# Two fp4 feed-forwards: VectorE's chains of x and of h woven into one another, x one turn ahead

## The chip, the cores and the metric

One core of one Trainium2 chip runs the whole program. The time is device microseconds of one execution. Of the kernel before there are three runs: 4086.76, 4089.36 and 4089.8 us, median 4089.36. Everything computes in fp32, except where the reference rounds to fp4.

## The reference

The program is a chain of eight sublayers on a residual stream of 8 sequences x 256 tokens x 128 channels, each with a layer norm in front. Two of the eight, the sixth and the last, are the same fp4 feed-forward with the same weights:

```python
def fp4_quant_dequant(x):                       # blocks of 16 along the last dim
    scale = max(max(abs(xb)) / 6.0, 1e-12)
    xn = xb / scale
    idx = searchsorted(_MID, abs(xn))            # 7 midpoints of the grid 0 .5 1 1.5 2 3 4 6
    return _GRID[idx] * sign(xn) * scale

gate = fp4_linear(x, w_gate)    # 128 -> 352, both operands rounded by blocks of 16
up   = fp4_linear(x, w_up)      # 128 -> 352
out  = fp4_linear(silu(gate) * up, w_down)       # 352 -> 128
```

Here x is the normed stream; out is added to the stream. The six other sublayers are not touched by the change.

## The kernel before, in words

The stream lies in SBUF for the whole program, channels on the 128 partitions (net.xT), its normed form likewise (net.zT). `fp4_ffn` goes over the 8 sequences ("images") one after the other, 256 tokens each, in a pipeline of stages that is written out by hand: each engine has one instruction list, in the order in which `iteration(n, stages)` appends it, and every engine waits for the others, and for its own earlier results, by semaphores. An engine's list is strictly in order.

The work of one image:

1. **x comes in** (TensorE, L2246): two transposes of net.zT bring tokens to the partitions, into x_in, one half of the bank p_x.
2. **The x chain** (VectorE, `round_x`): eight instructions, each of which waits for the one in front: maximum of each block (L2345), scale (L2348), reciprocal (L2350), the factor against ties (L2352), the quotients into SBUF (L2354, tile x_a) and once more in place in PSUM (L2356), their exponents (L2358), and from those the magic number (L2360) that rounds when it is added and subtracted.
3. **Rounding x** (GpSimd): moved = a + magic (L2130), q = moved - magic (L2132), xq = q x scale (L2137).
4. **x back** (TensorE, L2252): two transposes into x_back, the other half of p_x; ScalarE copies them to xqT (L2300).
5. **Up** (TensorE, L2260): four matmuls of 352 columns, two into the banks p_gate and two into p_up. ScalarE takes SiLU of the gate (L2305).
6. **The h chain** (VectorE): the product h = SiLU(gate) x up of 704 columns (L2366), block maximum (L2368), scale, reciprocal and tie factor of 44 columns (L2379 to L2383), quotients (L2385, tile h_a), exponents (L2387), magic number (L2389); each waits for the one in front. GpSimd makes h_moved and h_q (L2130 and L2132 again); VectorE scales back into hq (L2373, `scale_back`).
7. **Down** (TensorE): six transposes of hq into p_h and p_last (L2270), copied by ScalarE (L2310, L2311), then a matmul that adds the residual (L2275) and three of the weights (L2277) into the other half of p_last; ScalarE copies the sum to net.xT (L2315, `add`).

In turn n VectorE does: x chain of image n, product and maximum of n-1, scale-back of n-2, the rest of the h chain of n-1. GpSimd: x of n, then h of n-1. TensorE: x back of n, x in of n+1, transposes of h of n-2, up of n, down of n-2. ScalarE: `add` of n-3, copy of x of n, copies of h of n-2, SiLU of n. x in of n+1 waits for ScalarE's copy of x_back (both lie in p_x). The transposes of h wait for the `add` of the image before (both lie in p_last). A single scale tile per chain makes the next scale wait for the scale-back of the image before.

In front of the first call the weights are rounded and transposed; both calls begin with a layer norm. What follows the calls (the next norm, the store) needs the last image.

Of the kernel before, what the change touches and what calls it, by code (L numbers as in the profile page):

```python
# [20 lines left out]
ACT = mybir.ActivationFunctionType  # L21
ALU = mybir.AluOpType
# [2172 lines left out]
def fp4_ffn(net, tag):  # L2195
# [12 lines left out]
    with Mem(nc, tag) as m:  # L2208
# [6 lines left out]
        x_ = {n: m.sb(f"x_{n}", [P, w]) for n, w in (("scale", NX), ("inv", NX), ("a", L), ("magic", L), ("moved", L), ("q", L))}  # L2215
        h_ = {n: m.sb(f"h_{n}", [P, w]) for n, w in (("a", H2), ("expo", H2), ("magic", H2), ("moved", H2), ("q", H2))}
        p_x = m.ps("p_x", [P, BANK])
# [5 lines left out]
        x_in, x_back, h_last, p_out = p_x[:, 0:L], p_x[:, L:2 * L], p_last[:, 0:L], p_last[:, L:2 * L]  # L2223
# [3 lines left out]
        h_am, h_inv0, h_inv, h_scale = (own(L + 2 * NX + i * NHB, NHB) for i in range(4))  # L2227
# [6 lines left out]
        def pipeline(iteration):  # L2234

            for n in range(B + 3):
                iteration(n, tuple(stage for stage in (1, 2, 3, 4) if 0 <= n - stage + 1 < B))

        @block.tensor
        def _(pe):  # L2240
            def turn_in(n):
                if n >= B:
                    return
                need(pe, s["xqT_ready"], n)
                for t in range(2):
                    ins = nc.tensor.transpose(x_in[:, t * P:(t + 1) * P], net.zT[:, n, t * P:(t + 1) * P], net.ident[:, :])  # L2246
                ins.then_inc(s["z_turned"], 1)

            def turn_back(n):
                pe.wait_ge(sx["out"], n + 1)  # L2250
                for t in range(2):
                    ins = nc.tensor.transpose(x_back[:, t * P:(t + 1) * P], xq[:, t * P:(t + 1) * P], net.ident[:, :])  # L2252
                ins.then_inc(s["xq_turned"], 1)
# [26 lines left out]
            def iteration(n, stages):  # L2280
                if 1 in stages:
                    turn_back(n)
                    turn_in(n + 1)
                if 3 in stages:
                    turn_h(n - 2)
                if 1 in stages:
                    up(n)
                if 3 in stages:
                    down(n - 2)

            turn_in(0)
            pipeline(iteration)
# [3 lines left out]
        def _(act):  # L2296
            def copy_x(n):
                act.wait_ge(s["xq_turned"], n + 1)
                need(act, s["up_ready"], 2 * (n - 1))
                nc.scalar.activation(xqT[:, n % 2, :], x_back, ACT.Copy).then_inc(s["xqT_ready"], 1)  # L2300
# [16 lines left out]
            def iteration(n, stages):  # L2317
                if 4 in stages:
                    add(n - 3)
                if 1 in stages:  # L2320
                    copy_x(n)
                if 3 in stages:
                    copy_h(n - 2)
                if 1 in stages:
                    silu(n)

            pipeline(iteration)

        @block.gpsimd
        def _(pool):  # L2330
            def iteration(n, stages):
                if 1 in stages:
                    fp4_round(pool, nc.gpsimd, x_, sx, n + 1)
                    fp4_times_scale(pool, nc.gpsimd, x_, sx, n + 1, xq[:, :])
                if 2 in stages:
                    fp4_round(pool, nc.gpsimd, h_, sh, n)

            pipeline(iteration)

        @block.vector  # L2340
        def _(dve):
            def round_x(n):
                done = n + 1
                dve.wait_ge(s["z_turned"], done)
                nc.vector.tensor_reduce(x_am, in_blocks(x_in), AX.X, ALU.max, apply_absolute_value=True).then_inc(sx["am"], 1)  # L2345
                need(dve, sx["out"], n)
                dve.wait_ge(sx["am"], done)
                nc.vector.tensor_scalar(x_["scale"][:, :], x_am, 1.0 / 6.0, 1e-12, ALU.mult, ALU.max).then_inc(sx["scale"], 1)  # L2348
                dve.wait_ge(sx["scale"], done)
                nc.vector.reciprocal(x_inv0, x_["scale"][:, :]).then_inc(sx["inv0"], 1)  # L2350
                dve.wait_ge(sx["inv0"], done)
                nc.vector.tensor_scalar(x_["inv"][:, :], x_inv0, TIES_DOWN, None, ALU.mult).then_inc(sx["inv"], 1)  # L2352
                dve.wait_ge(sx["inv"], done)
                nc.vector.tensor_tensor(in_blocks(x_["a"][:, :]), in_blocks(x_in), per_block(x_["inv"][:, :]), ALU.mult).then_inc(sx["a"], 1)  # L2354
                dve.wait_ge(sx["a"], done)
                nc.vector.tensor_tensor(in_blocks(x_in), in_blocks(x_in), per_block(x_["inv"][:, :]), ALU.mult).then_inc(sx["turned_a"], 1)  # L2356
                dve.wait_ge(sx["turned_a"], done)
                nc.vector.tensor_scalar(x_expo.bitcast(U32), x_in.bitcast(U32), EXPONENT, None, ALU.bitwise_and).then_inc(sx["expo"], 1)  # L2358
                dve.wait_ge(sx["expo"], done)
                nc.vector.tensor_scalar(x_["magic"][:, :], x_expo, 1.0, MAGIC, ALU.max, ALU.mult).then_inc(sx["magic"], 1)  # L2360

            def multiply(p):
                done = p + 1
                dve.wait_ge(s["gated"], done)
                dve.wait_ge(s["up_ready"], 2 * done)
                nc.vector.tensor_tensor(h[:, :].rearrange("p (t f) -> p t f", t=2), gate[:, :, :], p_up[:, :, 0:DF], ALU.mult).then_inc(s["h_ready"], 1)  # L2366
                dve.wait_ge(s["h_ready"], done)
                nc.vector.tensor_reduce(h_am, in_blocks(h[:, :]), AX.X, ALU.max, apply_absolute_value=True).then_inc(sh["am"], 1)  # L2368

            def scale_back(r):  # L2370
                need(dve, s["h_turned"], r)
                dve.wait_ge(sh["q"], r + 1)
                nc.vector.tensor_tensor(in_blocks(hq[:, :]), in_blocks(h_["q"][:, :]), per_block(h_scale), ALU.mult).then_inc(sh["out"], 1)  # L2373

            def scale_h(p):
                done = p + 1
                need(dve, sh["out"], p)
                dve.wait_ge(sh["am"], done)
                nc.vector.tensor_scalar(h_scale, h_am, 1.0 / 6.0, 1e-12, ALU.mult, ALU.max).then_inc(sh["scale"], 1)  # L2379
                dve.wait_ge(sh["scale"], done)  # L2380
                nc.vector.reciprocal(h_inv0, h_scale).then_inc(sh["inv0"], 1)
# [238 lines left out]
```

## Time and profile before

| | |
|---|---|
| median of three runs | 4089.36 us |
| the profiled execution's own time | 4093.68 us |
| its span, in which the rows below count | 4091.9 us |
| busy: TensorE, VectorE, ScalarE, GpSimd | 3767.2, 3550.8, 3327.1, 3075.6 us |
| granted TensorE clock, mean | 0.965 of full |
| first fp4 call, first transpose to last residual copy | 3838.55 to 3927.51 us |
| second fp4 call, to its last residual copy | 3995.00 to 4084.27 us |

A row of the timeline has its start on the span's clock, its duration, the engine (PE is TensorE, DVE VectorE, ACT ScalarE, POOL GpSimd), the line of the kernel, the operation, the tile written and the tiles read, and shapes as partitions x columns. Tile names are cut: fp_p_own is the bank p_own, which holds the small tiles of both chains. In square brackets stands how long the engine had been idle and what released it. Merged rows give a count (x4) and the time from the first start to the last end.

### The profile page before, as it was taken

What the parts mean: (1) busy time and instruction counts of PE and PEld (TensorE: products, weight loads), DVE (VectorE), ACT (ScalarE), POOL (GpSimd) and SP (SyncE); (2) the same over time, 40 slices, a digit from 0 to 9 for tenths busy, and PEclk for the clock granted to TensorE, in tenths of its full rate; (3) what the DMA queues carried; (4) which work ended last, traced back from release to release, by engine and by line L of the source; (5) the groups of instructions that cost most, each with busy time, mean ns of one, the idle gap of its engine ahead of it and who ended that gap; (6) DMA issues with size and microseconds to landing.
All of it is one profiled execution on the core that took longest, in us unless ns stands there. A gap on an engine that the chain in (4) does not pass through costs nothing. (4 is left out here: it accounts for less than half of the span.)

```text
span 4091.9 us, 139809 instructions
## 1 busy us (share of the span) xinstructions
PE 3767.2 (92%) x51875; PEld 2247.0 (55%) x51875; DVE 3550.8 (87%) x11427; ACT 3327.1 (81%) x10473; POOL 3075.6 (75%) x4007
## 2 busy tenths in 40 slices
PE   6888889999999999999867999999999999996676
PEld 2333346666666666666553666666666666663464
DVE  7999989999999999999487999999999999975646
ACT  6888689999999999999515999999999999993122
POOL 3999788888888888888396888888888888762314
PEclk8999999999999999999898999999999999997887
DMA  1000111111112111111002111111111111110000
GB/s 30 1 1 1 48 25 34 44 34 39 44 28 54 31 36 49 26 36 34 12 1 64 26 36 46 29 50 35 31 48 35 44 31 39 31 26 3 6 3 11
DMA packets 78603, 122.65 MB, mean 30 GB/s; under 512 B 26024, under 2 KB 47204, under 8 KB 77924
## 3 DMA queue, kind: packets, MB, share of 16 engines
q1 hardware_dynamic: 77924, 113.71, 10.7%
q8 instruction: 413, 6.77, 0.7%
q14 instruction: 266, 2.18, 0.2%
HBM read 35.56 MB, written 1.05 MB: 9 GB/s over the span
## 5 line engine op out<-in xcount | busy, mean ns | idle before, releaser
L1131 POOL TENSOR_TENSOR local_qk<-local_qk,local_rb 128x512 f32<-128x512 f32 x768 | 973.2, 1278 | 88.5 <-DVE local_rb L1541 88.5
L1427 ACT ACTIVATE local_pr<-local_tb,local_nmax 128x96 f32<-128x96 f32 x3072 | 1010.5, 379 | 24.6 <-DVE local_nmax L1560 14.1
L1237 PE MATMUL local_pj<-local_wqkv,local_xs 128*64 128x512 f32 x3072 | 814.1, 609 | 21.5 <-DVE local_rb L1541 8.3
L1164 POOL TENSOR_TENSOR local_pr<-local_pr,local_rsum 128x384 f32<-128x384 f32 x768 | 623.0, 828 | 274.4 <-DVE local_rsum L1567 274.4
L1560 DVE CUSTOM_DVE_ANT_0 local_tb<-local_tb,local_mask,local_rinv 128x96 f32<-128x96 f32 x3072 | 772.6, 319 | 14.5 <-PE local_tb L1262 14.0
L1427 ACT ACTIVATION_READ_ACCUMULATOR local_pr<-local_tb,local_nmax 128x1 f32 x3072 | 753.1, 245 | 0.0
L1538 DVE TENSOR_TENSOR local_qk<-local_pj,local_rope 128x512 f32<-128x512 f32 x768 | 517.4, 674 | 113.7 <-ACT local_sq L1410 108.5
L1548 DVE TENSOR_REDUCE local_ss<-local_sq 128x8 f32<-128x512 f32 x768 | 521.8, 680 | 32.0 <-ACT local_sq L1410 32.0
L1410 ACT ACTIVATE local_sq<-local_pj 128x512 f32<-128x512 f32 x768 | 491.6, 640 | 55.6 <-PE local_pj L1237 55.3
L1541 DVE TENSOR_TENSOR local_rb<-local_pj,local_rope 128x512 f32<-128x512 f32 x768 | 523.0, 681 | 3.4 <-POOL local_qk L1131 3.4
L1286 PEld LDWEIGHTS local_ob<-local_prT,local_v 128*64 128x64 f32 x12288 | 413.9, 138 | 137.8 <-issue 55.4
L1435 ACT ACTIVATE local_prT<-local_tb 128x512 f32<-128x512 f32 x768 | 457.2, 639 | 5.7 <-PE local_tb L1273 5.7
L1560 DVE DVE_READ_ACCUMULATOR2_ANT local_nmax<- 128x1 f32 x3072 | 433.1, 141 | 0.0
L1286 PE MATMUL local_ob<-local_prT,local_v 128*64 128x64 f32 x12288 | 428.2, 223 | 3.4 <-DVE local_oT L1577 1.8
L1248 PE MATMUL local_pj<-local_wqkv,local_xs 128*64 128x512 f32 x1536 | 410.5, 613 | 4.4 <-DVE local_rb L1541 4.2
L1137 POOL TENSOR_TENSOR local_qk<-local_qk,local_rinv 128x512 f32<-128x512 f32 x384 | 400.5, 1044 | 0.0
L1262 PEld LDWEIGHTS local_tb<-local_kT,local_qT 64*64 64x64 f32 x12288 | 271.5, 133 | 202.9 <-ACT local_pr L1427 78.4
L783 POOL TENSOR_TENSOR mamba_scan_drive<-mamba_u,mamba_scan_b_all 128x512 f32<-128x512 f32 x256 | 319.8, 1271 | 52.3 <-ACT mamba_scan_b_all L753 48.7
L1311 PE MATMUL local_fb<-local_oT,local_wo 128*64 128x256 f32 x3072 | 348.0, 379 | 0.0
L1262 PE MATMUL local_tb<-local_kT,local_qT 64*64 64x96 f32 x12288 | 329.2, 250 | 3.3 <-ACT local_pr L1427 1.8
L1301 PEld LDWEIGHTS local_tb<-net_ident,local_qk 64*128 64x128 f32 x6144 | 231.5, 139 | 183.1 <-issue 82.3
L1350 PE MATMUL local_fb<-local_xn,local_w 128*64 128x256 f32 x2304 | 308.5, 389 | 10.3 <-DVE local_g L1601 5.7
(461 smaller groups left out, 7252.6 us busy)
## 6 DMA issues: line engine op xcount, KB each, us to landing
local_v<-local_v SPq DMA_DIRECT2D x288, 256.0 KB, 3.8
local_wqkv<-L_ffn_Wqkv_dram SPq DMA_DIRECT2D x72, 256.0 KB, 2.8
local_wo<-L_ffn_Wo_dram SPq DMA_DIRECT2D x12, 512.0 KB, 4.0
local_w<-L_ffn_W_dram SPq DMA_DIRECT2D x12, 341.0 KB, 2.9
mamba_parts<-mamba_in_low SPq DMA_DIRECT2D x24, 64.0 KB, 2.0
local_w<-L_ffn_W_dram SPq DMA_DIRECT2D x12, 128.0 KB
y_dram<-store_xtok SPq DMA_DIRECT2D x4, 256.0 KB, 2.8
local_oT<-rope_dram SPq DMA_DIRECT2D x2, 256.0 KB, 2.8
```

The costliest lines, as they stand in the source:

```text
L1131: nc.gpsimd.tensor_tensor(qk[:, u, :], qk[:, u, :], rb[:, u % 2, :], ALU.add).then_inc(s["summed"], 1)
L1164: nc.gpsimd.tensor_tensor(at, at, view(rsum[:, k // 2, k % 2, 0:1], [[1, 4], [0, KW]]), ALU.mult).then_inc(s["weighted"], 1)
L1237: ins = nc.tensor.matmul(bank[own, :], xs[:, par, u // 4 * P + own.start:u // 4 * P + own.stop], wqkv[:, dep % 2, u % 4 * BANK:(u % 4 + 1) ...
L1262: ins = nc.tensor.matmul(sc[h][low * QB:(low + 1) * QB, i * KW:(i + 1) * KW], qT[own, par, p, q:q + QB], kT[own, par, p, q:q + KW], start= ...
L1286: ins = nc.tensor.matmul(ob[h * DH:(h + 1) * DH, i * P + low * QB:i * P + (low + 1) * QB], v[:, par, V_BLOCK[2 * t + low], 2 * (4 * half + ...
L1410: nc.scalar.activation(sq[:, u % 2, :], projection_bank("rotated", u)[:, :], ACT.Square).then_inc(s["squared"], 1)
L1427: ins = nc.scalar.activation(pr[:, (NU * c + k) % PR_RING, i, WIN:WIN + KW], scores[:, i * KW:(i + 1) * KW], ACT.Exp, scale=-1.0, bias=nma ...
L1435: nc.scalar.activation(prT[:, kk % PT_RING, low, :], pair_of_banks("probs", kk)[low][:, :], ACT.Copy).then_inc(s["probs_copied"], 1)
L1538: nc.vector.tensor_tensor(heads8(qk[:, u, :]), heads8(bank[:, :]), cosines, ALU.mult)
L1541: nc.vector.tensor_tensor(rb[:, u % 2, :].rearrange("p (h a c) -> p h a c", a=2, c=DH // 2), swapped, sines, ALU.mult).then_inc(s["rotated ...
L1548: nc.vector.tensor_reduce(ss[:, par, 8 * u:8 * u + 8], heads8(sq[:, u % 2, :]), AX.X, ALU.add).then_inc(s["summed_sq"], 1)
L1560: ins = nc.vector.tensor_tensor_reduce(at, at, mask[:, k // 4, :], rinv[:, par, head:head + 1], 3.0e38, ALU.add, ALU.min, nmax[:, k, i:i + 1])
```

## The change

- **VectorE**: each step becomes a function of its own. Step by step an instruction of the h chain of image n-1 is followed by one of the x chain of image n+1; the scale-back of n-2 ends the turn. The x chain of image 0 runs alone ahead of the loop. Each step still waits for its own chain's previous step by the same semaphores; new waits guard the tiles that are reused: h quotients wait until h_moved of the image before has been made (`sh["moved"]`), h_magic until its q has (`sh["q"]`), likewise in the x chain.
- **GpSimd**: in turn n x of image n, then h of image n-2. h of an image waits for the scale-back of the one before; xq for the transposes back of the one before.
- **TensorE**: in turn n x in of n+1, transposes of h of n-3, x back of n, up of n, down of n-3. x in waits for the exponents of the image before in place of ScalarE's copy; x back waits for SiLU of the image before.
- **ScalarE**: copies of h of n-3, copy of x of n, SiLU of n, `add` of n-3.
- **Tiles**: x_back moves to the last 128 columns of both gate banks; the x scale is two SBUF tiles, the h scale two slices of p_own, taken in turns.

```diff
-        x_in, x_back, h_last, p_out = p_x[:, 0:L], p_x[:, L:2 * L], p_last[:, 0:L], p_last[:, L:2 * L]
+        x_in, x_back, h_last, p_out = p_x[:, 0:L], p_gate[:, :, BANK - P:BANK], p_last[:, 0:L], p_last[:, L:2 * L]
-        h_am, h_inv0, h_inv, h_scale = (own(L + 2 * NX + i * NHB, NHB) for i in range(4))
+        h_am, h_inv0, h_inv = (own(L + 2 * NX + i * NHB, NHB) for i in range(3))
+        h_scale = [own(L + 2 * NX + i * NHB, NHB) for i in (3, 4)]
...
             def turn_in(n):
-                need(pe, s["xqT_ready"], n)
+                need(pe, sx["expo"], n)
...
             def turn_back(n):
                 pe.wait_ge(sx["out"], n + 1)
+                need(pe, s["gated"], n)
...
+            for n in range(B + 3):
+                within(turn_in, n + 1)
+                within(turn_h, n - 3)
+                within(turn_back, n)
+                within(up, n)
+                within(down, n - 3)
...
+            for n in range(B + 3):
+                within(copy_h, n - 3)
+                within(copy_x, n)
+                within(silu, n)
+                within(add, n - 3)
...
+            def round_x(n):
+                fp4_round(pool, nc.gpsimd, x_, sx, n + 1)
+                need(pool, s["xq_turned"], n)
+                fp4_times_scale(pool, nc.gpsimd, {"q": x_["q"], "scale": x_scale[n % 2]}, sx, n + 1, xq[:, :])
+
+            def round_h(p):
+                need(pool, sh["out"], p)
+                fp4_round(pool, nc.gpsimd, h_, sh, p + 1)
+
+            for n in range(B + 2):
+                within(round_x, n)
+                within(round_h, n - 2)
...
+            def h_quotients(p):
+                dve.wait_ge(sh["inv"], p + 1)
+                need(dve, sh["moved"], p)
...
+            def h_magic(p):
+                dve.wait_ge(sh["expo"], p + 1)
+                need(dve, sh["q"], p)
...
+            for step in (x_max, x_scales, x_invert, x_ties, x_quotients, x_in_place, x_exponents, x_magic):
+                step(0)
+            for n in range(B + 2):
+                within(h_product, n - 1)
+                within(x_max, n + 1)
+                within(h_max, n - 1)
+                within(x_scales, n + 1)
+                within(h_scales, n - 1)
+                within(x_invert, n + 1)
+                within(h_invert, n - 1)
+                within(x_ties, n + 1)
+                within(h_ties, n - 1)
+                within(x_quotients, n + 1)
+                within(h_quotients, n - 1)
+                within(x_in_place, n + 1)
+                within(h_exponents, n - 1)
+                within(x_exponents, n + 1)
+                within(h_magic, n - 1)
+                within(x_magic, n + 1)
+                within(scale_back, n - 2)
```

`within(step, n)` calls the step where 0 <= n < 8.

## Rows read from the trace of the kernel before

**Rows 1.** Windows: the two fp4 calls, busy us of each engine, clock in the seventh field.
```profile
3838.50:3927.60 89.10, 58.15 (x209) 39.31 (x209) 64.40 (x136) 20.29 (x41) 43.05 (x40) 0.81 0.00 1
3995.00:4084.30 89.30, 58.87 (x209) 39.57 (x209) 64.41 (x136) 20.29 (x41) 43.02 (x40) 0.79 0.00 1
```

**Rows 2.** Waits of the first call: total us, times, longest.
```profile
...
DVE fp_p_own L2345 <- PE fp_p_x L2246: 8.7, 2, 4.5
...
DVE fp_h L2366 <- PE fp_p_up L2260: 4.4, 5, 1.5
...
```

**Rows 3.** Timeline, VectorE, one turn: start, duration, engine, line, operation, tiles.
```profile
3874.24 0.42 DVE L2345 TENSOR_REDUCE fp_p_own<-fp_p_x 128x16 f32<-128x256 f32 x1
...
3876.87 0.42 DVE L2360 TENSOR_SCALAR fp_x_magic<-fp_p_own 128x256 f32<-128x256 f32 x1
...
3877.21 0.88 DVE L2366 TENSOR_TENSOR fp_h<-fp_gate,fp_p_up 128x704 f32<-128x704 f32 x1
...
3881.73 0.53 DVE L2387 TENSOR_SCALAR fp_h_expo<-fp_h_a 128x704 uint32<-128x704 uint32 x1
...
3882.29 0.53 DVE L2389 TENSOR_SCALAR fp_h_magic<-fp_h_expo 128x704 f32<-128x704 f32 x1
...
3882.73 0.43 DVE L2345 TENSOR_REDUCE fp_p_own<-fp_p_x 128x16 f32<-128x256 f32 x1
```

**Rows 4.** Timeline, GpSimd, the same turn.
```profile
3874.40 1.67 POOL L2130 TENSOR_TENSOR fp_h_moved<-fp_h_a,fp_h_magic 128x704 f32<-128x704 f32 x1 [4.35 <-DVE fp_h_magic L2389]
...
3877.78 0.72 POOL L2130 TENSOR_TENSOR fp_x_moved<-fp_x_a,fp_x_magic 128x256 f32<-128x256 f32 x1
...
3879.38 0.62 POOL L2137 TENSOR_TENSOR fp_xq<-fp_x_q,fp_x_scale 128x256 f32<-128x256 f32 x1
```

**Rows 5.** Timeline, VectorE and GpSimd, local stage: one sum alone and beside GpSimd.
```profile
1833.35 0.43 DVE L1611 TENSOR_TENSOR net_xT<-net_xT,net_zT 128x256 f32<-128x256 f32 x1
...
1956.79 1.05 POOL L1137 TENSOR_TENSOR local_qk<-local_qk,local_rinv 128x512 f32<-128x512 f32 x1
...
1956.87 1.25 DVE L1611 TENSOR_TENSOR net_xT<-net_xT,net_zT 128x256 f32<-128x256 f32 x1
```

**Rows 6.** Timeline, first image of the first call: gate matmuls, then the product.
```profile
3846.28 2.55 PE L2260 MATMUL fp_p_gate<-net_w_gate_up,fp_xqT 128*128 128x352 f32 x4
...
3851.04 0.89 DVE L2366 TENSOR_TENSOR fp_h<-fp_gate,fp_p_up 128x704 f32<-128x704 f32 x1 [1.45 <-PE fp_p_up L2260]
```

**Rows 7.** Windows: one turn of the first call with a rest of TensorE.
```profile
3857.00:3866.00 9.00, 3.93 (x13) 2.99 (x14) 8.38 (x19) 1.25 (x3) 5.87 (x6) 0.71 0.01 2
```

**Rows 8.** Timeline, TensorE and ScalarE, a turn at the full clock.
```profile
3870.64 0.38 ACT L2300 ACTIVATE fp_xqT<-fp_p_x 128x256 f32<-128x256 f32 x1
...
3871.36 0.66 PE L2270 MATMUL fp_p_h<-net_ident,fp_hq 128*128 128x128 f32 x4
...
3872.07 1.35 PE L2260 MATMUL fp_p_gate<-net_w_gate_up,fp_xqT 128*128 128x352 f32 x4
...
3872.27 0.60 ACT L2310 ACTIVATE fp_hqT<-fp_p_h 128x512 f32<-128x512 f32 x1 [1.25 <-PE fp_p_last L2270]
...
3873.26 1.35 PE L2260 MATMUL fp_p_up<-net_w_gate_up,fp_xqT 128*128 128x352 f32 x4
...
3876.37 0.38 ACT L2315 ACTIVATE net_xT<-fp_p_last 128x256 f32<-128x256 f32 x1 [2.15 <-PE fp_p_last L2277]
```

**Rows 9.** Timeline, end of the first call, from the product of image 7.
```profile
3910.10 0.89 DVE L2366 TENSOR_TENSOR fp_h<-fp_gate,fp_p_up 128x704 f32<-128x704 f32 x1 [0.66 <-PE fp_p_up L2260]
...
3913.05 0.89 DVE L2373 TENSOR_TENSOR fp_hq<-fp_h_q,fp_p_own 128x704 f32<-128x704 f32 x1 [1.14 <-POOL fp_h_q L2132]
...
3919.32 0.38 ACT L2315 ACTIVATE net_xT<-fp_p_last 128x256 f32<-128x256 f32 x1 [3.55 <-PE fp_p_last L2277]
...
3921.48 0.66 PE L2270 MATMUL fp_p_h<-net_ident,fp_hq 128*128 128x128 f32 x4 [2.20 <-DVE fp_hq L2373]
...
3927.13 0.38 ACT L2315 ACTIVATE net_xT<-fp_p_last 128x256 f32<-128x256 f32 x1 [3.87 <-PE fp_p_last L2277]
```

More of the change, by code:

```diff
@@ L2214, in fp4_ffn @@
         hqT = m.sb("hqT", [P, 3, L])
[L2215 removed]
+        x_ = {n: m.sb(f"x_{n}", [P, w]) for n, w in (("inv", NX), ("a", L), ("magic", L), ("moved", L), ("q", L))}
         h_ = {n: m.sb(f"h_{n}", [P, w]) for n, w in (("a", H2), ("expo", H2), ("magic", H2), ("moved", H2), ("q", H2))}
+        x_scale = [m.sb(f"x_scale{i}", [P, NX]) for i in range(2)]
         p_x = m.ps("p_x", [P, BANK])
@@ L2232, in fp4_ffn, with within @@
         block = m.block()
-        def pipeline(iteration):
-            for n in range(B + 3):
-                iteration(n, tuple(stage for stage in (1, 2, 3, 4) if 0 <= n - stage + 1 < B))
+        def within(step, n):
+            if 0 <= n < B:
+                step(n)
         @block.tensor
@@ L2340, in _, with x_max, x_scales @@
+            def round_h(p):
[4 more added lines that the diff above has]
+                within(round_h, n - 2)
         @block.vector
         def _(dve):
-            def round_x(n):
-                done = n + 1
-                dve.wait_ge(s["z_turned"], done)
+            def x_max(n):
+                dve.wait_ge(s["z_turned"], n + 1)
                 nc.vector.tensor_reduce(x_am, in_blocks(x_in), AX.X, ALU.max, apply_absolute_value=True).then_inc(sx["am"], 1)
[L2346 to L2351, printed above, removed]
+            def x_scales(n):
+                dve.wait_ge(sx["am"], n + 1)
+                need(dve, sx["out"], n - 1)
+                nc.vector.tensor_scalar(x_scale[n % 2][:, :], x_am, 1.0 / 6.0, 1e-12, ALU.mult, ALU.max).then_inc(sx["scale"], 1)
@@ L2352, in round_x, with x_invert, x_ties, x_quotients @@
+            def x_invert(n):
+                dve.wait_ge(sx["scale"], n + 1)
+                nc.vector.reciprocal(x_inv0, x_scale[n % 2][:, :]).then_inc(sx["inv0"], 1)
+            def x_ties(n):
+                dve.wait_ge(sx["inv0"], n + 1)
                 nc.vector.tensor_scalar(x_["inv"][:, :], x_inv0, TIES_DOWN, None, ALU.mult).then_inc(sx["inv"], 1)
-                dve.wait_ge(sx["inv"], done)
+            def x_quotients(n):
+                dve.wait_ge(sx["inv"], n + 1)
+                need(dve, sx["moved"], n)
@@ L2366, in multiply, with h_max, h_scales @@
                 nc.vector.tensor_tensor(h[:, :].rearrange("p (t f) -> p t f", t=2), gate[:, :, :], p_up[:, :, 0:DF], ALU.mult).then_inc(s["h_ready"], 1)
-                dve.wait_ge(s["h_ready"], done)
+            def h_max(p):
+                dve.wait_ge(s["h_ready"], p + 1)
                 nc.vector.tensor_reduce(h_am, in_blocks(h[:, :]), AX.X, ALU.max, apply_absolute_value=True).then_inc(sh["am"], 1)
+            def h_scales(p):
+                dve.wait_ge(sh["am"], p + 1)
+                nc.vector.tensor_scalar(h_scale[p % 2], h_am, 1.0 / 6.0, 1e-12, ALU.mult, ALU.max).then_inc(sh["scale"], 1)
```

91 lines of the change are left out of this document (25 added, 66 removed).

## The prediction

> **What bounds the kernel now.** I read the windows of the two calls first: each takes 89 us, VectorE is busy for 64.4 of them, TensorE for 58, GpSimd for 43 [rows 1]. So the change can reach at most 178 of 4092 us. VectorE is the fullest engine, but not full. The waits of the first call say what it lacks: 8.7 us for transposed x at the start and 4.4 us for the up product in five stalls [rows 2]. The timeline then shows a turn without a stall, from one maximum of x to the next: 3874.24 to 3882.73, 8.49 us [rows 3]. VectorE never pauses visibly in it, and yet it is not dense. h_magic starts 0.56 us after the 0.53 us exponent step on whose result it waits (held: 0.03 us after the end); the maximum of x, which doesn't wait for h_magic, starts 0.44 us after it (free: 0.09 us before the end). x_magic and the product behind it show the same, 0.34 us apart at 0.42 us of duration [rows 3]. In the old order 14 of a turn's 17 starts are held and 3 are free. The bound is thus the sum of VectorE's steps with their held starts, plus stalls in about every other turn; seven turns, from the product of image 0 at 3851.04 to that of image 7 at 3910.10, take 59.06 us [rows 6, 9].
>
> **The woven chains.** No VectorE instruction is added or removed; h and x steps alternate, and the waited-for result is now two instructions old. Fourteen held starts become free: 14 x (0.03 + 0.09) = 1.7 us, 8.49 - 1.7 = 6.8. Twice a short x step is over before the result of the long h step in front of it is out (0.035 us each): 6.85 us. Let T be the end of x_magic in a turn. Before T + 6.85, the next such end, stand x_magic 0.42, h_magic 0.53, x exponents 0.43 and h exponents 0.53 with three overlaps: the h exponents start at T + 5.2. One h product (0.88 long, as the h quotients are, [rows 3]) and one x step earlier, at T + 4.05, stand the h quotients.
>
> **GpSimd beside it.** Its turn is now x first and then h: 2.22 us from 3877.78 to 3880.00 and 3.42 us from 3874.40 to 3877.82, 5.60 together, as in the block of [rows 4]. It starts 0.08 us after T. h_moved ends at T + 3.93, heard 0.1 us later: the new wait before the h quotients (queued behind it: both chains) is met at about the moment it is reached. q ends at T + 5.68, ahead of h_magic (T + 6) and of the scale-back (T + 6.8). So GpSimd has 1.2 us to spare. The second scale buffers are what lets it run late; they cost nothing, as no instruction comes with them.
>
> **A price that the old order never paid.** The h exponents and h_magic read and write 704 columns of SBUF in 0.53 us, while the product needs 0.88 [rows 3]; in the old order GpSimd was idle during both. In the new one the exponents start at T + 5.2, under q. What GpSimd does to a VectorE instruction on the same ground is shown by one sum of two SBUF tiles: 0.43 us alone, but 1.25 us beside a GpSimd instruction that runs to 1957.84, and it ends 0.28 us after that [rows 5]. Neither the 0.53 us form nor any of this size beside GpSimd stands in the trace. Bounds: nothing (it goes by as the product does), or the wait until q is over: end at 5.68 + 0.53 - 0.14 = T + 6.07 in place of 5.72, 0.35 us a turn. I take 0.35, by the row; above it, if h_magic were caught as well, 0.9. h_magic can't be caught where the timeline holds, since it waits for q and GpSimd then rests until the next T. Turn: 7.20 us.
> The Trainium skill states it as a rule (SBUF — State Buffer, Who interferes with whom): a VectorE instruction in a two-port mode, tensor_scalar from SBUF to SBUF among them, and a GpSimd instruction lock each other out for a whole instruction. It speaks against this change: by it the turn is the 7.20 us, without it 6.95; rows 5 agree with it for two SBUF inputs, and no row here for tensor_scalar.
>
> **TensorE and ScalarE.** Transposing back into the gate's banks frees the transposes of x from waiting for ScalarE's copy; the new wait, for SiLU of the image before, is long met (SiLU runs under the up half). What now stands in one line: transposes of h until their copy starts 0.91 us (3871.36 to 3872.27), that copy, in two parts, until the next can start 0.8 (0.60 for the larger one), copy of x 0.38 and 0.15 to the first matmul, gate and up 2.37 until down can start (3872.07 to 3874.44) and down with the residual copy until 3876.75, 2.31: 6.9 us at the full clock [rows 8]. That is under 7.20 but above 6.85: without GpSimd's price TensorE would bind, at 6.95. The product of image n finds its matmuls done at about T + 5.8, two us early; the old stalls on it go. Clock: it was 0.71 on the mean in a stretch in which TensorE worked 3.9 of 9 us [rows 7]. The new turns keep it at work for some 6 of 7.2 us (the line just added up without its copies, and the x transposes), with pauses near 0.5, and should run at the 2.4 GHz level. But turn 2 comes before h is in the loop: TensorE rests some 2 and 2.4 us around two transposes, and then gate and up run as in the first image, 4.7 us (3846.28 to 3851.04) instead of 2.54 [rows 6, 8]. They start at 9.8 us after product 0, so product 2 comes at 14.5 instead of 13.3: 1.2 us, once a call (bounds 0 and 2).
>
> **Start and end.** The transposes of image 1 no longer stand between the first copy and the first gate matmul: 0.45 us less. Tail: product 7 at H; the h chain alone keeps its held starts, 5.61 us from 3877.21 to 3882.82 less 0.80 for the scale-back in it, 4.8 [rows 3]; scale-back 6 at H + 4.75. From there the old tail needed 6.65 to the end of the residual copy (3913.05 to 3919.70), for which the last h transposes wait (one bank): H + 11.4; from those to the end 6.03 (3921.48 to 3927.51): H + 17.5, against 17.41 now [rows 9]. The earlier last scale-back (H + 9.3) is hidden by that wait. Nothing gained; up to 3 us if the clock stays up.
>
> **Sum for one call.** Product 0 to 1: 6.05 (a turn without scale-back and its 0.80, GpSimd at rest). Five turns of 7.20: 36.0. The last turn, h alone: 6.65, since q again ends the lock. Cold restart 1.2. Together 49.9 against 59.06: -9.15. Start -0.45, tail +0.1: -9.5. Two calls, the second as long as the first [rows 1]: -19.0 us. On the profiled execution's own time, 4093.7 (span 4091.9), this is 4074.7; that execution is 4.3 us above the median of the runs, 4089.4, so the median should be 4070.4, said as 4070.
>
> **Rivals.**
> A. Forecast, 4070: chance 0.55, own range 4066 to 4076.
> B. No price beside GpSimd and a warm clock: turns 6.95, no restart (1.2), tail 1.5 better: 9.5 + 5 x 0.25 + 0.3 + 1.2 + 1.5 = 13.7 a call, 4062. For it: VectorE's instructions with one SBUF operand ran beside GpSimd all through the old turns unstretched. 0.17.
> C. The woven steps pay more: lock 0.9 instead of 0.35, or satisfied double waits that cost some 0.05 in seven steps: turns 7.75, 5.5 x 0.55 = 3 less a call, 4077; both together 4082. 0.14.
> D. Weaving gains no overlap. The free starts that I count on are seen three times a turn, but behind waits that had been met for microseconds. If a start two behind its producer only follows the end of the one before: 8.21 + 0.35 a turn, 7.3 + 5 x 8.56 + 6.65 + 1.2 = 57.9, gain 1.1 + 0.35 a call: 4086.5. 0.08. The Trainium skill has a rule of this kind (VectorE: DVE Perf Modes, The DRAIN you can't avoid): the next instruction starts only when the pipe is empty, and semaphores between chained ones cost nothing; it would give this D, and the starts in rows 3, 0.44 behind 0.53 and 0.56 behind 0.53, contradict it.
> E. Slower: TensorE's strict order at the low clock. The new order puts both copies between its transposes and matmuls. At 1.2 GHz the line above is 6.03 (last h transposes to the end, [rows 9]) + 0.53 + 4.65 = 11.2 us, and it, not VectorE, sets the turn. Each such turn costs 4.0 us; from 2.4 more of them a call the kernel is slower, with all five 4.0 x 5 - 9.5 = 10.5 a call, 4110. For it: in the old turn with a long rest of TensorE the clock did fall [rows 7]. Against: only turn 2 has such rests. 0.06.
>
> **How the numbers follow.** The time is A's. The range reaches over B and most of C: 4060 to 4083. About 8 us (0.2%) is what a measurement of this kernel can tell from nothing, so faster means under 4081.2: A, B and most of C, 0.83; same: D and the rest of C, 0.11; slower: E, 0.06.
>
> **What would show it.** Products 7.2 us apart (6.95: B; 8.5: D; 11: E) in turns 3 to 6; VectorE starts 0.08 to 0.09 before the end of the one in front, with the same durations as now; the h exponents alone longer, near 0.9 us, and ending about 0.4 behind q; h_magic at 0.53; the clock at its upper level from image 3 on; last h transposes released by ScalarE's residual copy. Calls of about 80 us instead of 89. Wrong I would be if another step waits in the turn, above all the h quotients on h_moved, where I find no slack, or if the exponents are not stretched.

## The result: 4066.0 us against 4089.6, faster by 0.57%

The changed kernel takes 4066.01 us (median of 6 runs), the kernel before 4089.58 (6 runs): ratio 0.9943, 95% interval 0.9930 to 0.9956. That is inside the forecast's own range (4066 to 4076) at its lower edge. The profiled execution took 4066.17 us, its span is 4064.4, the mean granted clock 0.972.

Windows over the two calls of the changed kernel; the granted clock is the seventh field (before: [rows 1]):
```profile
3839.80:3915.20 75.40, 51.96 (x209) 33.95 (x209) 59.31 (x136) 20.40 (x41) 43.20 (x40) 0.91 0.00 1
3980.70:4057.20 76.50, 53.70 (x209) 34.90 (x209) 59.12 (x136) 20.40 (x41) 43.20 (x40) 0.87 0.00 1
```
VectorE shows fewer busy microseconds for the same 136 instructions (59.3 against 64.4 in call 1), since a stretch in which two of them overlap is counted once: by the timeline 99 of them start before the one in front has ended, where it was 15, and these overlaps are 6.6 us more. The other way, the instructions last 1.5 us longer in sum: the h exponents 2.4 more (below), the others a little less. The clock rose from 0.81 and 0.79 to 0.91 and 0.87; call 2 ran its first up half at the lower level too. The calls, cut into three parts (us; "run" is the time from product 0 to product 7):

| | first max of x to product 0 | run | product 7 to the end | call |
|---|---|---|---|---|
| before, call 1 / 2 | 11.76 / 12.01 | 59.06 / 58.81 | 17.41 / 17.65 | 88.23 / 88.47 |
| predicted, call 1 | 11.3 | 49.9 | 17.5 | 78.7 |
| changed, call 1 / 2 | 10.59 / 11.69 | 49.67 / 49.67 | 14.33 / 14.33 | 74.59 / 75.69 |

The spans differ by 27.5 us: 13.6 and 12.8 in the calls, 1.9 between them (68.3 to 66.4), and what lies ahead of and behind them took 0.9 longer. The medians differ by 23.6; the profiled execution of before was 4.3 above the median, that of the changed kernel 0.2. Windows between the calls, before and changed:
```profile
3927.60:3995.00 67.40, 56.91 (x420) 44.45 (x420) 22.26 (x47) 21.17 (x39) 2.94 (x4) 0.88 0.02 5
3915.20:3980.70 65.50, 54.96 (x420) 43.17 (x420) 22.27 (x47) 21.17 (x39) 2.95 (x4) 0.91 0.02 5
```
The same 420 matmuls kept TensorE busy for 2.0 us less, at a granted clock of 0.91 in place of 0.88; that the clock is the cause of the 1.9 fits, but no run tests it.

VectorE in a steady turn of call 1 (answers to [rows 3]):
```profile
3871.19 0.41 DVE L2368 TENSOR_SCALAR fp_x_magic<-fp_p_own 128x256 f32<-128x256 f32 x1
...
3872.32 0.87 DVE L2373 TENSOR_TENSOR fp_h<-fp_gate,fp_p_up 128x704 f32<-128x704 f32 x1
3873.12 0.42 DVE L2337 TENSOR_REDUCE fp_p_own<-fp_p_x 128x16 f32<-128x256 f32 x1
3873.45 0.87 DVE L2377 TENSOR_REDUCE fp_p_own<-fp_h 128x44 f32<-128x704 f32 x1
...
3875.20 0.41 DVE L2355 TENSOR_TENSOR fp_x_a<-fp_p_x,fp_x_inv 128x256 f32<-128x256 f32 x1
3875.72 0.89 DVE L2394 TENSOR_TENSOR fp_h_a<-fp_h,fp_p_own 128x704 f32<-128x704 f32 x1
3876.52 0.42 DVE L2359 TENSOR_TENSOR fp_p_x<-fp_p_x,fp_x_inv 128x256 f32<-128x256 f32 x1
3876.86 0.90 DVE L2398 TENSOR_SCALAR fp_h_expo<-fp_h_a 128x704 uint32<-128x704 uint32 x1
...
3878.02 0.51 DVE L2403 TENSOR_SCALAR fp_h_magic<-fp_h_expo 128x704 f32<-128x704 f32 x1
3878.45 0.41 DVE L2368 TENSOR_SCALAR fp_x_magic<-fp_p_own 128x256 f32<-128x256 f32 x1
...
3879.58 0.87 DVE L2373 TENSOR_TENSOR fp_h<-fp_gate,fp_p_up 128x704 f32<-128x704 f32 x1
```
The products are 7.26 us apart; in the other steady turns 7.25 to 7.27, but for the third of call 2, 6.91 behind a late one of 8.40. ("Pitch" below is this distance of products.) Each start lies 0.04 to 0.09 before the end of the one in front, except that the h quotients come 0.11 after the end of the x quotients. And one step is longer than it was: the h exponents last 0.90 instead of 0.53.

GpSimd, the same turn (answers to [rows 4]):
```profile
3873.94 1.67 POOL L2130 TENSOR_TENSOR fp_h_moved<-fp_h_a,fp_h_magic 128x704 f32<-128x704 f32 x1
3875.69 1.69 POOL L2132 TENSOR_TENSOR fp_h_q<-fp_h_moved,fp_h_magic 128x704 f32<-128x704 f32 x1
```
h_moved ends at 3875.61; the h quotients, which wait for it, start 0.11 later. q ends at 3877.38, the h exponents at 3877.76, 0.38 later. How long they last depends on how much of q is left, and the distance from its end to theirs does not: here are the last turn of call 1 and the third of call 2, VectorE and GpSimd:
```profile
3897.48 1.68 POOL L2132 TENSOR_TENSOR fp_h_q<-fp_h_moved,fp_h_magic 128x704 f32<-128x704 f32 x1
3898.43 1.11 DVE L2398 TENSOR_SCALAR fp_h_expo<-fp_h_a 128x704 uint32<-128x704 uint32 x1
```
```profile
4010.50 1.68 POOL L2132 TENSOR_TENSOR fp_h_q<-fp_h_moved,fp_h_magic 128x704 f32<-128x704 f32 x1
4011.84 0.73 DVE L2398 TENSOR_SCALAR fp_h_expo<-fp_h_a 128x704 uint32<-128x704 uint32 x1
```
1.11 and 0.73 long, they end 0.38 and 0.39 after q.

The second turn of call 1, all engines (answers to [rows 6, 7]):
```profile
3859.44 1.67 POOL L2130 TENSOR_TENSOR fp_h_moved<-fp_h_a,fp_h_magic 128x704 f32<-128x704 f32 x1
3860.45 2.72 PE L2261 MATMUL fp_p_gate<-net_w_gate_up,fp_xqT 128*128 128x352 f32 x4 [0.47 <-ACT fp_xqT L2295]
3861.22 0.89 DVE L2394 TENSOR_TENSOR fp_h_a<-fp_h,fp_p_own 128x704 f32<-128x704 f32 x1 [0.89 <-POOL fp_h_moved L2130]
```
The end of call 1, ScalarE, VectorE and TensorE (answers to [rows 9]), and then the clock of a window in it:
```profile
3905.55 0.88 DVE L2408 TENSOR_TENSOR fp_hq<-fp_h_q,fp_p_own 128x704 f32<-128x704 f32 x1
...
3909.96 0.89 DVE L2408 TENSOR_TENSOR fp_hq<-fp_h_q,fp_p_own 128x704 f32<-128x704 f32 x1 [3.53 <-POOL fp_h_q L2132]
3910.34 0.38 ACT L2310 ACTIVATE net_xT<-fp_p_last 128x256 f32<-128x256 f32 x1 [2.08 <-PE fp_p_last L2278]
...
3910.90 0.66 PE L2271 MATMUL fp_p_h<-net_ident,fp_hq 128*128 128x128 f32 x4 [0.60 <-DVE fp_hq L2408]
...
3913.27 1.46 PE L2278 MATMUL fp_p_last<-fp_hqT,net_w_down 128*128 128x256 f32 x6
```
```profile
3905.00:3909.00 4.00, 2.03 (x12) 1.32 (x11) 1.39 (x3) 1.25 (x3) 2.42 (x2) 1.00 0.00 0
```

### The profile page after: what moved, and what is told of

Its sections match the earlier page's. It is cut to its first block and busy times, and to the rows that moved or that the text cites. A ratio compares the mean times of both kernels' runs of the same rounds, so it can differ in the third digit from the quotient of the medians.

```text
span 4064.4 us, 139891 instructions
## 1 busy us (share of the span) xinstructions
PE 3752.0 (92%) x51875; PEld 2235.5 (55%) x51875; DVE 3540.4 (87%) x11427; ACT 3327.3 (82%) x10473; POOL 3080.5 (76%) x4007
## 3 DMA queue, kind: packets, MB, share of 16 engines
q14 instruction: 266, 2.18, 0.2%
## 5 line engine op out<-in xcount | busy, mean ns | idle before, releaser
L1560 DVE CUSTOM_DVE_ANT_0 local_tb<-local_tb,local_mask,local_rinv 128x96 f32<-128x96 f32 x3072 | 772.2, 317 | 14.4 <-PE local_tb L1262 13.9
```

The costliest lines, as they stand in the source:

```text
L1560: ins = nc.vector.tensor_tensor_reduce(at, at, mask[:, k // 4, :], rinv[:, par, head:head + 1], 3.0e38, ALU.add, ALU.min, nmax[:, k, i:i + 1])
```

## The experiments

Ratios are to the kernel before, run in turn on the same chip, with 95% intervals; "pitch" is the distance of products in steady turns, the "start" of a call is from the first maximum of x to product 0, its "tail" from product 7 to the end, in the profiled execution. The experiments ran on three chips, on which the median of the kernel before was 4089.19 (e1, e3, e4, e6), 4096.78 (e2, e5, e7, e8) and 4087.55 us (e9 to e12), two tenths of a per cent apart: compare ratios across them, not times. A "held" start is one that waits for the instruction right in front, as in the prediction; a "free" one waits for an earlier one. Orders of steps are given in short.

**e1, the woven order undone.** All else as changed, x still one turn ahead.
```diff
-  h_product, x_max, h_max, x_scales, h_scales, ... h_magic, x_magic, scale_back
+  h_product, h_max, h_scales, ... h_magic, x_max, x_scales, ... x_magic, scale_back
```


> The changed kernel, but VectorE runs the h chain of a turn whole and then the x chain whole; order of images, GpSimd, TensorE, ScalarE, tiles all as in the changed kernel. Theory (the gain of the turns is the held starts that weaving frees): 14 held starts come back, 8.5 us a turn, and the h quotients and exponents now meet GpSimd's h_moved and q about a microsecond too early, so products stand 9.4 to 9.7 us apart and the kernel takes 4088 to 4094 us, no better than before the change. Rival (x one turn ahead makes the gain, the weaving nothing): products stay 7.3 us apart, 4066.

Measured 4091.42 us, ratio 1.0003 (0.9994 to 1.0012): the whole gain is gone. Pitch 9.61, calls 88.02 and 89.20; the seven turns take 63.19 us in each, against 59.06 before and 49.67 changed. GpSimd and VectorE in one turn of it:
```profile
3880.67 1.67 POOL L2130 TENSOR_TENSOR fp_h_moved<-fp_h_a,fp_h_magic 128x704 f32<-128x704 f32 x1
...
3882.41 1.68 POOL L2132 TENSOR_TENSOR fp_h_q<-fp_h_moved,fp_h_magic 128x704 f32<-128x704 f32 x1
3882.44 0.89 DVE L2394 TENSOR_TENSOR fp_h_a<-fp_h,fp_p_own 128x704 f32<-128x704 f32 x1 [0.62 <-POOL fp_h_moved L2130]
3883.36 1.12 DVE L2398 TENSOR_SCALAR fp_h_expo<-fp_h_a 128x704 uint32<-128x704 uint32 x1
```
So the lead of x alone costs: GpSimd's work on h moves under VectorE's h chain, which then waits 0.62 for h_moved and pays 0.59 in the exponents (9.61 - 8.49 = 1.1 a turn). The weaving takes off 9.61 - 7.26 = 2.35 (13.5 in the seven turns). A comparison of before and after shows only their difference. The tails of e1 are 14.34 and 14.33: what keeps the clock up there is not the weaving.

**e8, only the banks**, in the kernel before: turned-back x in the gate's banks, so that x of the next image is turned in ahead of it, with the waits that go with it (x in for the exponents, x back for SiLU, xq for the transposes back).
```diff
-        x_in, x_back, h_last, p_out = p_x[:, 0:L], p_x[:, L:2 * L], p_last[:, 0:L], p_last[:, L:2 * L]
+        x_in, x_back, h_last, p_out = p_x[:, 0:L], p_gate[:, :, BANK - P:BANK], p_last[:, 0:L], p_last[:, L:2 * L]
...
-                need(pe, s["xqT_ready"], n)
+                need(pe, sx["expo"], n)
...
+                need(pe, s["gated"], n)
...
-                    turn_back(n)
                     turn_in(n + 1)
+                    turn_back(n)
```


> The kernel before the change with one part of it: x turned back into the gate's banks, transposes of the next x before the transposes back and waiting for the exponents only. VectorE's order is the old one. Theory (this part only frees TensorE from waiting for ScalarE's copy): the first gate matmuls 0.45 us earlier a call, and up 0.45 earlier where TensorE is late, in three or four turns: 1.5 to 2.5 us a call, 4085 to 4087. Rival (banks carry most of the gain): below 4080.

Measured 4089.69 against 4096.78, ratio 0.9986 (0.9977 to 0.9996). Calls 85.72 and 86.23, 2.4 less on the mean; the pitches are 8.5 to 8.95 instead of 8.5 to 10.1, since product stalls are gone; of the 2.5 in call 1, 1.2 is the start, in which the up half ran at the upper level. Alone it is worth 4.7 us in the two calls, under a fifth of what the whole change saves there (26.4). The medians differ by 7.1, and their interval takes in both.

**e2, one x scale** instead of two: the scale of the next x waits for xq.
```diff
-x_scale = [m.sb(f"x_scale{i}", [P, NX]) for i in range(2)]
+x_scale = [m.sb("x_scale", [P, NX])] * 2
...
-                need(dve, sx["out"], n - 1)
+                need(dve, sx["out"], n)
```


> The changed kernel with one x scale tile instead of two: the next x scale waits for GpSimd's xq of the image before. Theory (xq ends 2.3 us after x_magic, the scale step comes 2.7 us after it, so the wait is met): products stay 7.26 us apart, 4065 to 4067. Rival (the second buffer is part of the gain): a wait of some 0.1 to 0.5 us a turn in front of the x scale, 4068 to 4074.

Measured 4070.38, ratio 0.9933 (0.9918 to 0.9948), pitch 7.25: the second buffer does nothing. (The time is above the 4065 to 4067 expected, on a chip whose kernel before is 7 us above the first.) xq is done 0.27 us before the next scale is reached: 3873.36 + 0.62 against 3874.25 in the changed kernel.

**e9, x woven in, but not ahead**: x of n beside h of n-1, no x chain ahead of the loop; GpSimd, TensorE and ScalarE take h one turn earlier too.
```diff
-                within(x_max, n + 1)       # and the seven steps behind it
+                within(x_max, n)
-                within(round_h, n - 2)
+                within(round_h, n - 1)
-                within(turn_h, n - 3)      # likewise down, copy_h, add
+                within(turn_h, n - 2)
```


> The changed kernel with the same woven order of VectorE, but x(n) woven with h(n-1) of the same turn instead of one turn ahead (x_max to x_magic of n instead of n + 1; no x chain ahead of the loop). Everything else as changed. Theory (x must be a turn ahead): x_magic ends 0.4 before the end of the 17-instruction turn, and only then may GpSimd take x: moved 0.8, q 0.8, xq 0.6, then turn back 0.5, copy 0.4, gate and up 2.8 with the gate's silu inside, together about 5.7, during which VectorE has only the scale-back (0.87) to do: turn 7.3 - 0.9 + 5.7 = 12 to 12.5 us a product, five more us in each of about seven turns, +33 to +37 a call, so 4130 to 4145 in all. Rival (weaving alone brings the gain, the lead of x is a matter of order): products 7.3 to 8.5 apart and a time of 4066 to 4085.

Measured 4174.89, ratio 1.0213 (1.0195 to 1.0232), 30 to 45 us above what was expected: the mechanism holds, the turn is 13.6 to 14.8 us, not 12 to 12.5. Waits over call 1, then a gate matmul and the clock of a stretch:
```profile
DVE fp_h L2373 <- PE fp_p_up L2261: 59.7, 8, 8.0
```
```profile
3879.64 2.71 PE L2261 MATMUL fp_p_gate<-net_w_gate_up,fp_xqT 128*128 128x352 f32 x4 [0.49 <-ACT fp_xqT L2295]
```
```profile
3865.00:3880.00 15.00, 7.75 (x21) 4.34 (x22) 6.77 (x17) 2.28 (x5) 6.77 (x6) 0.61 0.00 1
```
VectorE waits for the up product in every turn. TensorE, which rests 5.4 us while the chains run, was granted 0.61 (mostly the 1.2 GHz level), and gate and up of one image took 3.9 to 5.1 us (5.1 for the gate shown), instead of 2.6. I had priced them at 2.8.

**e7, q made for half of the columns**: it leaves out h_q of the second 352 columns (zeros there), so that GpSimd is at rest when the h exponents come.
```diff
-                fp4_round(pool, nc.gpsimd, h_, sh, p + 1)
...
+                nc.gpsimd.tensor_tensor(h_["q"][:, 0:DF], h_["moved"][:, 0:DF], h_["magic"][:, 0:DF], ALU.subtract).then_inc(sh["q"], 1)
```


> The changed kernel with half of q left out: GpSimd subtracts for the first 352 columns of h only, the other half of q is zero, so that the instruction takes 0.85 instead of 1.69 us. Theory (exponents are held until q ends): q ends 0.85 us earlier, before the exponents start plus 0.14, and they take 0.52 to 0.55; the h quotients still wait for h_moved; turn 6.95 to 7.0. Rival (GpSimd's presence in the turn slows VectorE's fast form in general): near 0.9.

One run, 4069.72 us (0.9934 of before). GpSimd and VectorE of one turn:
```profile
3877.34 0.93 POOL L2330 TENSOR_TENSOR fp_h_q<-fp_h_moved,fp_h_magic 128x352 f32<-128x352 f32 x1
...
3878.50 0.52 DVE L2402 TENSOR_SCALAR fp_h_expo<-fp_h_a 128x704 uint32<-128x704 uint32 x1
```
All 16 exponent steps took 0.52 or 0.53. The time didn't fall: this execution had gate and up at 2.2 and 2.3 us in turns where the changed kernel has 1.45 and 1.35, and pitches from 6.2 to 8.7. For the stretched exponents it is clean, for their price in the total it is not.

**e3 and e4, order of steps.** Both put the in-place x step before the h quotients and the x exponents before the h exponents; e4 also puts x_magic before h_magic. Nothing else differs.
```diff
-  x_quotients, h_quotients, x_in_place, h_exponents, x_exponents, h_magic, x_magic
+  x_quotients, x_in_place, h_quotients, x_exponents, h_exponents, h_magic, x_magic   # e3
+  x_quotients, x_in_place, h_quotients, x_exponents, h_exponents, x_magic, h_magic   # e4
```


> The changed kernel with VectorE's order turned in four places: x in place before the h quotients, x exponents before the h exponents, h_magic straight behind the h exponents (one held start). Theory (the h exponents at 0.90 instead of 0.53 us and the h quotients 0.19 us late are waits for GpSimd's q and h_moved): the h quotients wait no more, the exponents start 0.3 later and end where they ended, at 0.55 us of duration, and products stand 6.95 us apart (now 7.26), 4062 to 4064. Rival 1 (the exponents are slowed by any GpSimd work beside them, not held until an instruction ends): they stay near 0.9 and the turn near 7.25, 4066. Rival 2 (TensorE's line of transposes, copies, matmuls is the bound already): products wait for the up matmuls, 7.2 us apart, 4066.

> As the kernel with x exponents before h exponents, but x_magic before h_magic, so that no start is held; h_magic (0.51 us, SBUF to SBUF) then runs where GpSimd wants to begin its turn. Theory (whoever starts first keeps the other out): h_magic stays 0.51, GpSimd's first x step starts or ends about 0.4 us later than now, which it can afford; VectorE's sum is 6.85, so TensorE's line of 6.95 sets the turn: 4062 to 4064. Rival (the lock falls on VectorE whatever the order): h_magic near 0.9, turn 7.2, 4066.

e3: 4067.1, ratio 0.9943 (0.9931 to 0.9955), pitch 7.04. That is not the 4062 to 4064 expected: the exponents take 0.62 (still 0.38 behind q), h_magic, again right behind its producer, is held, 0.10 + 0.12 above e4, and the tails are 15.85 and 15.67 at a lower clock, which takes back what the turns won. e4: 4059.8, ratio 0.9930 (0.9918 to 0.9941), pitch 6.81, calls 74.05 twice: 2 to 4 us below the 4062 to 4064 expected, in part because TensorE's 6.95 did not bind. Its turn is not free of held starts, as its expectation says: x in place stands right behind the x quotients and starts 0.04 after their end. Without the stretched exponents (0.37) and the late h quotients (0.19) the changed order would come to 7.26 - 0.56 = 6.70, an estimate; the held start puts 0.12 back. Rows of this kernel are shown with its repeat below.

**e5 and e6, the clock at both ends.** Matmuls on spare data: e5 in the kernel before, six ahead of each of the last two turns of h and six at the end; e6 in the changed kernel, five and four ahead of the first gate.
```diff
+                if n >= B:                                   # e5
+                    pe.wait_ge(s["gated"], B)
+                    pe.wait_ge(s["h_ready"], B)
+                    warm(nc, net, p_gate[:, 0, :], 6)
...
             turn_in(0)
+            warm(nc, net, p_gate[:, 0, :], 5)                # e6
...
+                if n == 0:
+                    warm(nc, net, p_gate[:, 0, :], 4)
```


> The kernel before the change with 6 idle bf16 matmuls on TensorE before each of the last two sets of h transposes and once more at the end of a call. Theory (the tail of the changed kernel is 14.3 instead of 17.4 and 17.7 us because the clock is at its upper level there): with the clock held up, the old tail falls to about 14.8, both calls together 5 us less, 4084. Rival (the tail is shorter since the order is another): the tail stays 17.4 or grows by the matmuls, 4089 or more.

> The changed kernel with nine idle bf16 matmuls of 512 columns on TensorE before the first up matmuls of each call, in its rests during the first x chain (their results are overwritten). Theory (the first gate and up run at 1.2 GHz since TensorE rested, 2.7 + 1.5 to 2.5 us instead of 2.5 together): from the first maximum of x to the first product 9.4 us instead of 10.6 and 11.7, the clock in that stretch well above 0.55, 4062 to 4064. Rival (the clock doesn't rise in so short a stretch, or the product waits for something else): no change, 4066.

e5: 4095.87, ratio 0.9995 (0.9986 to 1.0005), tails 17.41 and 15.86: not the 5 us less that were expected. In call 1 the clock fell all the same, as its window shows:
```profile
3924.00:3928.00 4.00, 4.00 (x10) 2.68 (x11) 0.00 (x0) 0.38 (x1) 0.00 (x0) 0.50 0.00 0
```
There the last down took 2.77 us; in call 2, with the clock back up in time, 1.46, and the tail was 1.8 shorter. That shows the price of the clock in a tail, not why the changed kernel keeps it.

e6: 4063.07, ratio 0.9936 (0.9924 to 0.9947). Call 1 began with a gate at the lower level all the same (start 10.39). Call 2 began at the 2.4 GHz level, start 9.01 instead of 11.69:
```profile
3987.66 1.45 PE L2261 MATMUL fp_p_gate<-net_w_gate_up,fp_xqT 128*128 128x352 f32 x4 [0.47 <-ACT fp_xqT L2298]
```
but its tail was 15.96 instead of 14.33: of 2.7 us, 1.6 were given back. The medians of e6 and the changed kernel are not told apart.

**e11, e12, e10: the changed kernel again, e4 again, and e4 with matmuls on spare data** (five and four ahead of the first gate, three ahead of the last two turns of h), beside one another on one chip. e11 and e12 carry no edit of their own.

> The changed kernel itself, run beside the others so that they compare on one chip: 0.9935 to 0.995 of before. [...]

> The swapped order of h quotients, exponents and h_magic alone, once more, beside the changed kernel on the same chip. Theory (the lock of 0.37 a turn is gone and the h quotients no longer wait 0.19 for moved): products 6.8 apart in the four steady turns, against 7.25: 4 times 0.45 = 1.8, less up to 0.5 of start and end, a call, so 2.5 to 3.6 below the changed kernel, 0.9992 to 0.9994 of it. Rival (the gain in the first look was the chip's spread): within 1 us of the changed kernel.

> The changed kernel with two edits that each gave something alone: h quotients, h exponents and h_magic each one place later on VectorE (the in-place step and the x exponents go ahead of them, so that the exponents start after GpSimd's q and are not held), and matmuls on spare data before the first gate of a call (5 and 4) and three ahead of each of the last two turns of h. Theory (the two are independent: one acts on the turns, the other on the start by the granted clock): products 6.8 apart, start 10.4 and 9.0, tails 14.3, so 1.5 to 2.5 below the swapped order alone, 0.992 of before, and 0.9980 to 0.9990 of the changed kernel on this chip. Rival (they share one thing, the clock of the stretch after the start, and the warm matmuls delay the first gates): same as the swapped order alone within 0.5 us, or the tail falls to half clock again in one call and gives 1.5 back.

| | median us | ratio, interval | calls in the profile |
|---|---|---|---|
| e11 changed | 4067.7 | 0.9952 (0.9939 to 0.9964) | 75.70, 75.68 |
| e12 swapped | 4059.7 | 0.9938 (0.9925 to 0.9952) | 72.25, 72.42 |
| e10 swapped, warm | 4059.57 | 0.9931 (0.9918 to 0.9943) | 70.98, 73.32 |

e11 lies just above the 0.9935 to 0.995 that were expected. GpSimd, VectorE and ScalarE in a turn of e12:
```profile
3875.41 0.38 ACT L2310 ACTIVATE net_xT<-fp_p_last 128x256 f32<-128x256 f32 x1 [2.15 <-PE fp_p_last L2278]
...
3878.10 0.41 DVE L2355 TENSOR_TENSOR fp_x_a<-fp_p_x,fp_x_inv 128x256 f32<-128x256 f32 x1
...
3878.36 1.68 POOL L2132 TENSOR_TENSOR fp_h_q<-fp_h_moved,fp_h_magic 128x704 f32<-128x704 f32 x1
...
3878.55 0.43 DVE L2359 TENSOR_TENSOR fp_p_x<-fp_p_x,fp_x_inv 128x256 f32<-128x256 f32 x1
...
3880.02 0.52 DVE L2398 TENSOR_SCALAR fp_h_expo<-fp_h_a 128x704 uint32<-128x704 uint32 x1
...
3880.78 0.52 DVE L2403 TENSOR_SCALAR fp_h_magic<-fp_h_expo 128x704 f32<-128x704 f32 x1
...
3880.95 0.94 POOL L2130 TENSOR_TENSOR fp_x_moved<-fp_x_a,fp_x_magic 128x256 f32<-128x256 f32 x1 [0.92 <-DVE fp_x_magic L2368]
...
3882.41 0.38 ACT L2310 ACTIVATE net_xT<-fp_p_last 128x256 f32<-128x256 f32 x1 [2.15 <-PE fp_p_last L2278]
```
The exponents start as q ends (3880.04) and are not stretched (in turn 2 and in the last turn they still start under q, and take 0.89 and 1.11). x in place (3878.55) is the held start. Now GpSimd pays instead: its x_moved starts under h_magic and takes 0.94 where it took 0.73. It has the time. Of the 3.4 us a call between e11 and e12 the steady turns give 1.4 and the last one 0.2, and turn 1 costs 0.1: 1.5 a call, 3.0 in all, is the order's share. The rest, start (1.2 and 1.0) and turn 2 (0.9), less 0.2 in the tail, goes with the clock of that execution; e4's own profile has them at 11.69 and 8.26. So the turns gave what was expected, and the time did not: e12 lies 8.0 us below e11, where 2.5 to 3.6 were expected, and e4 6.2 below the changed kernel's 4066.01, both more than that share. The intervals of the ratios overlap, so how much of it is the order stays open.
e10 and e12 are equal, where e10 was expected 1.5 to 2.5 lower. The starts came out at 9.02 and 9.01 (expected: 10.4 and 9.0), and the time didn't follow: turn 2 took 0.4 and 1.0 longer than in e12, and in call 2 a late gate ran at the lower level and the last turn took 7.43 instead of 6.48.
```profile
4031.05 2.61 PE L2261 MATMUL fp_p_gate<-net_w_gate_up,fp_xqT 128*128 128x352 f32 x4 [1.01 <-ACT fp_xqT L2302]
```
The rival was right: what the clock won at the start was missing later.

## Why the prediction was right, and where its steps were not

- **Woven chains, 6.85 us a turn: right.** e4's turn has no wait for another engine and no stretched step: 6.81, with one start still held; with all of them free it would be some 6.7 (an estimate, at e4). e1 shows that nothing else carries the gain of the turns.
- **The lock, 0.35 on the h exponents: right**, 0.37 by the rows (0.90 against 0.53), end 0.38 behind q where the sum had 0.39 (5.68 + 0.53 - 0.14 = 6.07). The Trainium skill's rule (SBUF — State Buffer, Who interferes with whom), which rows 5 could show only for two SBUF inputs, holds for this tensor_scalar too: e7, e4 and e12 take the neighbour away in the steady turns and the step is back at 0.52. That GpSimd is held in turn is seen in e12.
- **Turn 7.20: measured 7.26.** The 0.06 is GpSimd's: with T = 3871.60 (end of x_magic) its q ended at T + 5.78, not T + 5.68, and the end of the exponents hangs on it. So the turn is a loop through GpSimd: 5.78 from x_magic to the end of q, 0.38 to the end of the exponents, 1.10 from there to the next x_magic (3878.86). The "1.2 us to spare" of the prediction were spare only towards the scale-back; towards the exponents GpSimd had nothing in hand. The wait of the h quotients for h_moved, which the prediction had named as a sign of being wrong, exists (0.19). By this loop it costs nothing here: without it the exponents would start earlier under the same q and be stretched by as much more. That is argued, not tested; the rows of call 2 above show such a trade in the other direction.
- **Free starts (rival D): fell.** The same 17 instructions, with the semaphores of their chains in both, take 8.49 us with 14 held starts and 6.81 with one: 0.13 for each start freed. What the Trainium skill states on semaphores between chained instructions, that they cost nothing (VectorE: DVE Perf Modes, The DRAIN you can't avoid), does not carry over to this chain: a wait for the instruction right in front has a price.
- **Product 0 to 1, 6.05, and the cold restart, 1.2: the place right, the partner missing.** 5.89, then 8.04 and 8.40, together 13.9 and 14.3 where 14.5 was forecast. Gate and up of image 2 did run cold (2.72 for the gate). But in call 1 product 2 came 0.52 after they were done: the h quotients had waited 0.89 for h_moved, because turn 1 has no scale-back in it, VectorE is 0.8 earlier, and GpSimd, whose turn stays the same, is not. What I booked as gained in turn 1 was only lent.
- **TensorE's line, 6.9 us, "would bind at 6.95": size right, conclusion wrong.** In e4 and e12 the residual copies are 7.00 us apart, and the products 6.81. TensorE falls behind by 0.2 a turn, but has about two us in hand (2.18 in e4, 1.37 by the last steady turn), and eight images are over before they are spent. A call is not an endless loop.
- **The tail, 17.5: wrong, and the largest miss.** The sum took the old clock: 6.65 from scale-back 6 to the end of the residual copy, 6.03 from the last transposes. With the clock at 1.00 throughout these were 5.17 and 4.24, and since the bank is free at 3910.72, the last transposes now wait for the scale-back (ended 3910.85), which I had called hidden. 3.2 us a call, 6.3 in all: the forecast had it as "up to 3 us if the clock stays up", without a chance of its own. In seven of the eight calls of the changed kernel, e2, e6 and e11 the tail is 14.33 or 14.34. Over all profiles it goes with the turn in which TensorE takes h: in the ten kernels that take h of n-3, both of the last downs ran at the upper level (1.46 or 1.47 us) in 17 of 20 calls; in the four that take h of n-2 (before, e5, e8, e9) in none of 8. Why is open, and e3, whose order differs from that of the changed kernel in two places, lost it in both calls (15.85 and 15.67).
- **Start, -0.45: -1.2 and -0.3.** In call 1 the gate took 2.71 and the up half 1.46 us, in call 2 both ran at the lower level (2.71 and 2.55); e6 shows what is in it (2.7 us).
- **Rival E fell for the changed kernel.** e9 shows one part of it, TensorE falling to the low clock when it rests in each turn, but not its line of TensorE as the bound: TensorE rests 5.4 us of a turn there. e9 is 87 us above before; of those the clock makes some 26, an estimate: what gate and up of 14 images took above 2.64 each. Most of the rest is the x chain, which comes a turn too late.

Sum for call 1: run -9.4, start -1.2, tail -3.1, against -9.15, -0.45 and +0.1. On the profiled execution's own time the forecast was 4074.7, and 4066.2 was measured: of the 8.5, 6.3 are the tails and 1.9 lie between the calls. For the median, 4070.4 against 4066.0, half of that was made up by the 4.3 I took off, which the changed kernel's profiled execution does not need (0.2). That is luck: without it the error would be twice as large. The turns were forecast by their mechanism; that the median still lies within A's own range owes something to this.

## What to carry to other kernels

Where an engine runs a chain of short dependent instructions, its busy time hides a cost at each start: compare a held start with a free one in the trace, and multiply. To weave in a second chain it must be ready a turn ahead, which moves another engine's work: price that move (lock, new waits) by itself, then shift the two or three steps that collide. When a step is taken out of one turn, ask whether its partner engine got faster too, else the gain is only lent to the next turn.

## What the runs showed that I had not expected

- VectorE's exponents step beside GpSimd's q: length between 0.62 and 1.12 us by when it starts, its end 0.37 to 0.39 us after GpSimd's in every case in which it was stretched. It works in the other direction too: x_moved 0.94 instead of 0.73 beside h_magic.
- The clock at the start of a call differs between executions of one kernel (start 10.6 or 11.7 in the changed kernel, 10.5 in e12, 11.7 in e4), and what spare matmuls won there was partly missing later in the same call (e6, e10).
